# Four graph layers on one core: a 300-wide memset ahead of each gather in five edge passes, 16 TensorE columns in the typed pass, last rows gathered straight into place

## The reference, cut to what matters

```
h = relu(layernorm(x)); x = x + GAT2(GAT1(h))        # attention, 3 heads, then 1
h = relu(layernorm(x)); x = x + log_softmax(RGCN1(RGCN0(h)))   # 8 relation types
h = relu(layernorm(x)); x = x + relu(h + sheaf(h))   # a small MLP per edge
h = relu(layernorm(x)); x = x + typed(h)             # 90 relation types
```

## Time and profile before

| | us |
|---|---|
| Median of 3 runs | 33200.59 |
| Lowest and highest of them | 33169.5, 33225.65 |
| Profiled execution, its time | 33120.21 |
| Its span | 33118.5 |

### The profile page before, as it was taken

The page is one execution under the profiler, slowest core; times in us unless marked ns, Lnnn a source line. Parts: engine busy times, 40 slices in busy tenths (PEclk is TensorE's granted clock), DMA queues, the critical chain, the costliest instruction groups (busy, mean ns, idle before and its releaser), DMA issues. The chain is left out here.

```text
span 33118.5 us, 433539 instructions
## 1 busy us (share of the span) xinstructions
PE 19164.6 (58%) x155012; PEld 15014.2 (45%) x155012; DVE 15783.7 (48%) x40197; ACT 1449.8 (4%) x3069; POOL 20831.6 (63%) x22292
## 2 busy tenths in 40 slices
PE   0565655588884555553777739899898892100000
PEld 0344444244443444443666628888888882000000
DVE  3444444455554444443666636667666663211110
ACT  0000000000000000000000001111111110000000
POOL 2544444566663444444888856888888885577776
PEclk9777777699996777776888869999999995555555
DMA  4111111111111100100111112222222223311111
GB/s 68 43 42 39 41 41 43 25 37 39 37 39 25 22 20 20 22 20 19 28 24 26 24 20 33 38 36 38 38 35 39 38 35 48 77 20 19 19 20 16
DMA packets 1707135, 1084.73 MB, mean 33 GB/s; under 512 B 1291531, under 2 KB 1565931, under 8 KB 1672139
## 3 DMA queue, kind: packets, MB, share of 16 engines
q0 software_dynamic: 934304, 199.11, 9.7%
q1 hardware_dynamic: 661867, 435.33, 5.6%
q10 hardware_dynamic: 110016, 437.07, 3.4%
HBM read 607.13 MB, written 462.62 MB: 32 GB/s over the span
## 5 line engine op out<-in xcount | busy, mean ns | idle before, releaser
L879 PE MATMUL gat_e_found<-gat_e_parts,gat_e_lowhot 128*128 128x266 bf16 (+1 forms) x36456 | 6298.0, 327 | 2542.1 <-issue 2386.8
L692 POOL DMA_INDIRECT rgcn_e_rows<-rel_t,rgcn_e_index x4464 | 4285.4, 960 | 3253.4 <-DMA rgcn_e_rows<-rel_t,rgcn_e_index 2449.1
L2039 POOL DMA_INDIRECT bysrc<-sheaf_e_toadd,sheaf_e_torow x3224 | 5182.0, 1607 | 1356.3 <-issue 862.3
L879 PEld LDWEIGHTS gat_e_found<-gat_e_parts,gat_e_lowhot 128*128 128x128 bf16 x36456 | 3645.3, 101 | 5194.3 <-issue 3397.1
L2278 PE MATMUL sheaf_e_found<-sheaf_e_parts,sheaf_e_lowhot 128*128 128x238 bf16 x46872 | 5310.3, 274 | 1003.3 <-DVE sheaf_e_lowhot L2090 523.7
L961 POOL DMA_INDIRECT gat_e_rows<-att_t,gat_e_index x4712 | 4464.7, 948 | 1999.1 <-issue 1510.8
L2278 PEld LDWEIGHTS sheaf_e_found<-sheaf_e_parts,sheaf_e_lowhot 128*128 128x128 bf16 x46872 | 4699.8, 102 | 1459.8 <-issue 641.5
L1769 PE MATMUL rgcn_e_found<-rgcn_e_parts,rgcn_e_lowhot 128*128 128x224 bf16 x41664 | 4424.5, 271 | 7.1 <-DVE rgcn_e_lowhot L1622 7.1
L1769 PEld LDWEIGHTS rgcn_e_found<-rgcn_e_parts,rgcn_e_lowhot 128*128 128x128 bf16 x41664 | 4163.0, 103 | 548.4 <-issue 398.6
L692 POOL DMA_INDIRECT typed_e_rows<-typed_t,typed_e_index x3224 | 3424.9, 1062 | 1074.1 <-issue 1060.6
L843 DVE TENSOR_TENSOR gat_e_picked<-gat_e_found,gat_e_highhot 128x532 f32<-128x532 f32 (+1 forms) x868 | 763.5, 880 | 4230.8 <-DMA count_rows<-dst_d,count_index 2071.6
(11 more groups left out here) (459 smaller groups left out, 20331.6 us busy)
## 6 DMA issues: line engine op xcount, KB each, us to landing
sheaf_e_allsrc<-src_d ACTq DMA_DIRECT2D x62, 1664.0 KB
sumsatt<-gat_e_sums ACTq DMA_DIRECT2D x62, 1404.0 KB
gat_e_rows<-att_t,gat_e_index POOLq DMA_INDIRECT x4712
typed_t<-typed_p_y SPq DMA_DIRECT2D x98, 765.0 KB
rgcn_e_rows<-rel_t,rgcn_e_index POOLq DMA_INDIRECT x4464
sheaf_e_low<-low_d SPq DMA_DIRECT2D x62, 1152.0 KB
sumsatt<-gat_e_sums ACTq DMA_DIRECT2D x62, 1092.0 KB
rgcn_e_low<-low_d SPq DMA_DIRECT2D x124, 512.0 KB
```

The costliest lines, as they stand in the source:

```text
L692: pool.indirect_dma_start(self.rows[k][:, j, :], None, table, rows(self.index[k][:, j:j + 1]))\
L879: last = pe.matmul(self.found_ps[n % 2][:, c, 0:self.width * NHI], hot[:, k, col * P:(col + 1) * P], self.table.column(part, k), start=par ...
L2039: pool.indirect_dma_start(g.by_src[k][r], rows(to_row[k][:, j:j + 1]), to_add[k][:, j, 0:FD], None, compute_op=ALU.add).then_inc(summed[k] ...
```

## The change

- `Pause.rest` puts a memset of 128x300 on POOL ahead of each gather, with a wait for the memset before it. All five passes use it; the element of gat1, the landing waits of gat2 and rgcn0 and the 400-wide memset of rgcn1 go.
- The typed pass finds 16 of 52 columns on TensorE. A found column gives `h[src]` and the source's part of the weight (17 values); `look` picks the type's 16x16 matrix by a one-hot of the type (3 matmuls of 256 columns per edge column), and `apply` multiplies and reduces on DVE (512 products for two columns). DVE's list for this pass is written anew, in the same form as in gat1.
- `project`: for wide tables ACT copies the first of the three banks. `parts` has two columns, and its store is contiguous (partition-major), with an index `dst_first_p` to fit.
- `gather_to` issues its 98 gathers straight into the result, without DVE; in the sheaf layer they run beside the loads of the eight tables, which DVE adds to each other first.

```diff
+PAUSE = 300
 def gather_to(nc, g, name, table, index, width, into):
-    gather_by_node(nc, g, name, table, index, width, copy, 2)
+            def _(pool):
+                gather_nodes(pool, table, index, width, into, got)
+                pool.wait_ge(got, 16 * NT)
+def gather_nodes(pool, table, index, width, into, got):
+    for t in range(NT):
+        pool.indirect_dma_start(into[:, t, 0:width], None, table, rows(index[:, t:t + 1])).then_inc(got, 16)
...
 # project
-                        for n in range(banks):
+                        for n in range(1 if shares else 0, banks):
...
+                def copy_first(i, k):
+                    act.wait_ge(product[k], i + 2)
+                    act.wait_ge(stored[k], i * 16 + 16)
+                    act.copy(rows_out[k][:, 0, 0:pieces[0][4]], y_ps[k][0][:, 0:pieces[0][4]])\
+                        .then_inc(first_copied[k], 1)
...
-                        sp.dma_start(by_node(node_table), keep[0][:, :, :]).then_inc(by_node_out, 16)
+                    sp.dma_start(node_table.rearrange("(p t) w -> p t w", p=P), keep[0][:, :, :])\
+                        .then_inc(by_node_out, 16)
...
+class Pause:
+    def rest(self, pool, n, first=False):
+        if not first:
+            pool.wait_ge(self.over, n)
+        pool.sem_inc(self.g.gate, 1)
+        pool.memset(self.cells[:, :], 0.0).then_inc(self.over, 1)
...
 # EdgeBuffers.gather_chunk: rgcn0, rgcn1
-            if self.space == "landed" and j > 0 and j % 2 == 0:
-                pool.wait_ge(self.gathered[k], turn * (16 * self.cols) + 16 * j)
-                pool.sem_inc(g.gate, 1)
-            elif self.space == "time":
...
-                pool.memset(self.spacer[:, :], 0.0).then_inc(self.spaced, 1)
+            self.pause.rest(pool, (turn * 2 + k) * self.cols + j, isinstance(turn, int) and turn == 0 and k == 0 and j == 0)
             self.gather_column(pool, table, k, j)
...
 # attention_pass: gat1, gat2
-                        if not kinds:
...
-                            pool.memset(spacer[:, :], 0.0).then_inc(spaced, 1)
-                        elif j % 8 == 0 and j > 0:
-                            pool.wait_ge(gathered[a.k], a.turn * (16 * JG) + 16 * j)
-                            pool.sem_inc(g.gate, 1)
+                        pause.rest(pool, a.c * JG + j, fresh and a.k == 0 and j == 0)
...
 # finish_sheaf
+            def _(pool):
+                gather_nodes(pool, g.sums["sheaf"], g.last_row, FD, agg, got)
...
+                for n in range(1, len(tables)):
+                    dve.wait_ge(in_[n], 16)
+                    o.link(dve.tensor_tensor(total, total, parts[n][:, :, :], ALU.add))
+                dve.wait_ge(got, 16 * NT)
...
+class TypedFinder(Finder):
+    def build_low(self, dve, a, q, fresh=False):
...
+        dve.tensor_scalar(self.type_hot[(a.k * self.groups + q) % 2][:, :],
+                          self.type_rows[a.k][:, q * QC * P:(q + 1) * QC * P], self.g.lane_f[:, :], None, ALU.is_equal)
+        super().build_low(dve, a, q, fresh)
+    def look(self, pe, a, n, first=False):
...
+            for part in range(3):
+                last = pe.matmul(self.kind_ps[n % 2][:, c, :, :].rearrange("p o i -> p (o i)"),
+                                 hot[:, col * P:(col + 1) * P], ...)
+    def apply(self, dve, o, a, n, rows_t, fresh=False):
...
+        o.link(dve.tensor_tensor(self.mapped[:, :, :, :], self.kind_ps[n % 2][:, :, :, :],
+                                 rows_t[a.k][:, j:j + 2, 0:FD].unsqueeze(2).to_broadcast([P, 2, FD, FD]), ALU.mult))
+        dve.tensor_reduce(rows_t[a.k][:, j:j + 2, 0:FD], self.mapped[:, :, :, :], AX.X, ALU.add)\
+            .then_inc(self.applied, 1)
...
 # typed_attention_pass, DVE, in the turn of chunk a (old = a-1)
+                    for n in range(f.halves):
+                            f.fetch(dve, o, a, n, rows_t, first, last)
+                        if fetches and n > 1:
+                            f.apply(dve, o, a, n - 2, rows_t, fresh=first and n == 2)
...
+                        if n == 0: begin(o, old)
+                        elif n == 1: weigh(o, old)
+                        elif n == 2: scale(o, old)      # waits for old's gathers, frees its rows
+                        else: add_up(o, old, n)
```

More of the change, by code:

```diff
@@ L552, in _ @@
                         last.then_inc(turned_sb[k], 1)
+                        if shares and not (first and k == 0):
+                            copy_first(i - 1 + k, 1 - k)
+                turn(0, first=True)
+                with act.Fori(1, turns) as i:
+                    turn(i)
+                if shares:
+                    copy_first(turns - 1, 1)
             @block.sync
@@ L588, in _ @@
                 pool.sem_inc(g.gate, 1)
-                pool.indirect_dma_start(first[:, :], None, node_table, rows(g.dst_first[:, :])).then_inc(got, 16)
+                first_node = g.dst_first_p if put_kept and node_table is not table else g.dst_first
+                pool.indirect_dma_start(first[:, :], None, node_table, rows(first_node[:, :])).then_inc(got, 16)
                 pool.wait_ge(ready, 1)
@@ L1542, in relation_pass @@
     with Stage(nc, name) as s:
-        b = EdgeBuffers(s, g, FD, index_d, extras, FD, JP, "landed" if first else "time")
+        b = EdgeBuffers(s, g, FD, index_d, extras, FD, JP)
         short = SplitTable(s, [h[:, :, :]], FD)
@@ L2611, in _ @@
                 o = Order(dve, dve_o)
+                dve.memset(raw[:, :, :], 0.0).then_inc(cleared, 1)
                 dve.memset(dst_part[1][:, :], 0.0)
[L2613 to L2641 removed]
@@ new lines, in add_up @@
+                def add_up(o, a, step):
+                    k = a.k
+                    if step == 3 and not a.is_first():
+                        dve.wait_ge(stored[k], a.turn * 16)
+                    steps = last_step - 2
+                    for c in range((step - 3) * FD // steps, (step - 2) * FD // steps):
+                        last = scan_sum(dve, sums[k][:, :, c], keep_ps, scaled[:, :, c],
+                                        sums[1 - k][:, J - 1, c:c + 1])
+                    if step == last_step:
+                        o.link(last)
+                        dve.sem_inc(done, 1)
@@ new lines, in _, with turn @@
+                o = Order(dve, dve_o, (NCH // 2 - 2) * per + base)
+                turn(o, At(NCH // 2 - 1, 1), last=True)
+                turn(o, At(NCH // 2, 0), fetches=False)
+            @block.tensor
+            def _(pe):
+                pe.wait_ge(f.table.ready, 1)
+                pe.wait_ge(f.kinds_ready, 1)
+                def turn(a, first=False):
+                    for n in range(f.halves):
+                        f.find(pe, a, n, first)
+                        f.look(pe, a, n, first)
+                turn(At(0, 0), first=True)
+                turn(At(0, 1))
+                with pe.Fori(1, NCH // 2) as i:
+                    for k in range(2):
+                        turn(At(i, k))
```

273 lines of the change are left out of this document (200 added, 73 removed).

## The result

The changed kernel took 29,630.6 us (median of 3, 29,597 to 29,786), the kernel before 33,200.6: ratio 0.893, 95% interval 0.889 to 0.897. The forecast was 28,770. The profiled execution took 29,786, where the sum gave 28,695: 1,091 us are missing, and the traces say where.

A forecast was written before the change was run, and what follows sets the result against it. Gathers on POOL and PE's matmuls, stalled beside rapid gathers, added up in gat1; POOL bound rgcn1. Terms summing to -4425 took the profiled 33,120 to 28,695, hence 28,770 us for the median; range 28,350 to 30,000.

The forecast's parts named there:

- main case: Whole kernel: POOL's pace sets all five passes, 28,770 us, within 28,400 to 29,100; chance 0.68.
- rival B: In gat1 and typed PE is partly held back, losing 12 us a chunk each: 30,260 us; chance 0.10.
- I take full speed: In the five passes PE keeps its full matmul speed at the smallest new gather spacing, 1.475 us.
- Rival A: PE is still held back at 1.475 us spacing in all five passes: 39,600 us, slower than before; chance 0.05.
- The pace: POOL in the passes: 1.519 us a gather, chunk starts included, with a 300-element memset of an estimated 371 ns.
- typed: Typed pass: 58.0 us a chunk at 1.611 us a gather, 3596 us for 4485, a gain of 889.
- lower bound of the pace: Typed pass: 1.519 us a gather instead of 1.611, if the longer gather does not stay; 3390 us.
- Rival C: Typed pass: PE and DVE bound it in turn, 66 us a chunk, 29,270 us in all; chance 0.12.
- Rival D: PE's stalls come from its own two-chunk loop, not from gathers: 32,960 us; chance 0.02.
- Small parts: Outside the passes' main gathers: projection -50, one-word store -50, last rows -66, sheaf -100 us.

The follow-up runs named there:

- first chip: Chip of the main result: kernel before 33,200 us, changed kernel 29,630 us.
- fourth chip: Another chip: kernel before 33,242 us, unchanged changed kernel 29,711 us, ratio 0.893.
- second chip: Another chip: kernel before 33,101 us in its profiled run (elsewhere 33,087), unchanged changed kernel 28,599 us, ratio 0.865.
- third chip: Another chip: kernel before 30,270 us; the changed kernel ran there only with memsets of 400, 350 or 200 elements, or without gathers.
- fifth chip: Another chip: kernel before 30,171 us; one variant of the changed kernel ran there, 28,849 us.
- half: Changed kernel with one-element memsets and gathers of 64 rows instead of 128 in gat1 and gat2 only: 37,248 us.
- p1: Changed kernel with `PAUSE = 1`, the memset before each gather at one element instead of 300: 36,919 us.
- mix: Changed kernel with memsets of 350 elements in gat1, rgcn0, rgcn1 and typed, 300 in gat2: 28,849 us, ratio 0.956 to the kernel before.
- the loop alone: Changed kernel with the five passes' gathers replaced by memsets, the 300-wide memsets kept: 24,857 us.
- 200: Changed kernel with memsets of 200 elements instead of 300: 27,439 us on the third chip, 34,225 us on the fourth chip.
- 350: Changed kernel with memsets of 350 elements instead of 300: 28,947 us on the third chip, 29,108 us on the fourth chip.

## Why the prediction was right, and where not

29,630 us lies in the range of 28,350 to 30,000, the direction was right, and the kernel gained 3,570 us of the 4,430 forecast. The mechanism was right where nothing holds TensorE back: there POOL's pace sets the end of all five passes. But the main case, 28,400 to 29,100 with a chance of 0.68, is not what the first chip did; the range held since it had been drawn over a milder rival B as well, and which chip the kernel met was luck: 28,599 on another, the main case.

Median matmuls a us between neighbouring gathers, by spacing (what a pass takes when nothing holds it: 8.6 to 8.8 in gat1, about 10 in rgcn; "by eights" is with a wait for landing after each eight, and gat2 asks for little more than it gets there):

```
gathers apart   first and fourth chip            second chip         third and fifth chip
1.25 us         0.8 (gat1 before; half: rgcn)    0.8 (p1, all)       not profiled
1.25, by eights 4.8 (gat2 before)                4.8 (gat2 before)   not profiled
1.395-1.399     2.15 (all five passes)           not run             8.6 gat1, 10.0 rgcn
1.478           5.3-5.4 gat1, 5.4 rgcn           8.6 gat1, 6.1 rgcn  4.7 (gat2 of mix)
1.52            8.5 gat1, 7.1-7.2 rgcn           not run             8.5 gat1, 7.9-8.6 rgcn
1.56            8.3 (rgcn1 before)               8.3 (rgcn1 before)  8.3 gat1, 8.3-8.8 rgcn
```

- **The step that failed is "I take full speed"** at 1.475 us, and behind it the thought that a row near to the good one decides. What was lost between 1.25 and 1.56 doesn't come back in proportion: on chips of the first kind the median is 1, 3 and 8 matmuls a gather at 1.25, 1.395 and 1.478 us, and enough only at 1.52. The margin had also to be read against the need: gat2's calm at an average of 1.52 proved little, since it asks for 4.1 matmuls a us and the others for 6.1 to 7.0, and since its landing waits break the run of gathers: without them, at `PAUSE = 1`, it gets 0.8 a us.
- **The price** is the 1,096 us of POOL's waits, 3.6, 4.6, 4.1 and 5.5 us a chunk in gat1, rgcn0, rgcn1 and typed. This is rival B in kind, a partial hold, with other numbers: it had 12 us a chunk in two passes, and it was four passes with a third to a half of that. 30,260 was too long, 28,770 too short.
- **Rival A** did not come true at 1.478 us. Its mechanism, the gathers and then TensorE alone, is there at 1.25 us (`PAUSE = 1`, 36,919 us): 79 to 82 us a chunk and 88 in gat2, where A, with the longer gathers of the pause in it, had 88 to 92 and 102. At 1.395 on the fourth chip the kernel is slower than before, at 71.8 to 75.3 us a chunk.
- **The pace** was right: 1.524 to 1.527 for 1.519, memsets 373 ns for 371.
- **The main case is the second chip's run.** From its own profiled run of the kernel before, 33,101 - 4425 = 28,676; it took 28,591. gat1 -1464 (forecast -1495), rgcn0 -1506 (-1570), rgcn1 -188 (-191), gat2 +14 (-14), typed -1060 (-889).
- **typed**: the longer gather (1.062 us) did not stay: 0.971 at 1.478 us from the same table, 0.972 at 1.395 and 0.947 at 1.25. So it was neither the table nor the pace; in the pass before, with nothing between the gathers, single ones take 0.94 or 1.09, and why is open. The lower bound of the pace was named and not taken, and that cost 187 us. VectorE is busy 2583 us, not 2700; the loop alone takes 43.8 us a chunk, not 48. Rival C is out by that, and by 55.2 us a chunk on the second chip.
- **Rival D** is out: the stalls follow the gathers' spacing in the same loop. The instruction queue in the profile's part 3 moves 680 packets in the changed kernel and 682 in the one with 1.25 us, so it is not more fetching either; whether a fetch takes longer beside the gathers, no run shows. The Trainium skill, Runtime: NRT & Kernel Launch, section Instruction fetch mechanics, says that refills in order are mostly hidden and that branches out of the window stall; the trace agrees as far as the packets go, and the rule has no stall at each gather.
- **Small parts** (second chip): from the last gather of one pass to the first of the next (in sheaf the last scatter), and from typed's last to the end, 2,304 us for 2,622, the stretch ahead of gat1 15 longer: -303, forecast -266. The last rows brought 17, 16 and 29 (22 each), sheaf to typed 152 (200). Missed were 60 and 43 behind gat1 and gat2: before, TensorE still had 60 and 42 us of finds left when POOL had gathered the last chunk (TensorE held back, as in the earlier trace rows). On the first chip these tails came back in rgcn0, rgcn1 and typed (24 to 31 us each), which ate the small parts' gain there.

Two groups of lines on POOL, second chip, between sheaf and typed (count, busy, mean ns, idle before): the last rows' gathers and the wait for the contiguous store:

```profile
L310 POOL DMA_INDIRECT sheafn_agg<-sumssheaf,whole_lastrow x98 | 100.0, 1020 | 32.5 <-issue 29.6 <-PEq L2481 3.0
...
L630 POOL DMA_INDIRECT typed_p_first<-typed_dst,whole_dstfirstp x1 | 1.0, 980 | 8.3 <-DMA typed_dst<-typed_parts 8.3
```

The gathers idle 32.5 us in all where those of the same place idled 51.9 before on this chip, but each takes 1.02 us for 0.946. The store's wait is 8.3 us for 51.2 before on this chip (53.0 on the first): -43, with -50 forecast.

**Open.** What is shared between a gather's start and TensorE's supply of instructions is not known; the runs show only that it does not go by rows or bytes, and that it sets in after some gathers of an unbroken run. Nor is it settled that it is the chip: the second to fifth are four different ones, none met twice, so a condition that lasts as long as a set of runs (rival M) would look the same. Within a set the runs of the kernel before agree within 0.2%. That the third chip's 2,930 us lie in gat1 and rgcn0 is inferred: the kernel before was not profiled there. And which pause is best depends on it: 200 wins by 5% over 350 where nothing is held back (27,439 to 28,947), and loses 18% where it is. 350 is the one tried on both the third and the fourth chip that lets no chunk wait on either; it did not run on the second.

## What to carry to other kernels

When the profile puts an engine's idle time down to `issue` in pieces that repeat with another engine's instruction, count the instructions that it gets in each period, and compare that with what the stage needs: a rate against a need says which stages will suffer, a "good" and a "bad" spacing do not. A pause tuned near such an edge should be tried on several chips, and the margin be priced (here 0.042 us a gather, 1.7% of the time) against what falls off the edge (up to 18%). A duration that differs between two stages (0.97 and 1.06 us) is not yet one of the data; look for its cause, or carry both ends into the sum.

## What the runs showed of the hardware

- Beside an unbroken run of indirect gathers from GpSimd, TensorE gets its instructions late, on some chips: medians of 1, 3 and 8 matmuls a gather at 1.25, 1.399 and 1.478 us (first and fourth chip), and 1 also with 64 rows instead of 128, at 1.21 us (same packets, fewer bytes). The portions come 0.74 us apart at 1.478, half the spacing.
- It takes a few gathers to set in: at 1.25 us the first six of a chunk in gat1 leave 9 to 11 matmuls each, then 0 to 2; with a wait for landing after each eight, gat2 keeps a median of 6.
- The spacing from which it happens differs: 1.478 us is held on the first and the fourth chip and nearly free on the second; 1.395 is free on the third and held on the fourth (1.399). The kernel before took 30,171 to 33,242 us on five chips.
- A gather of 64 rows takes 0.907 us on GpSimd on average (gat1 and gat2 of that run), one of 128 rows 0.950 (the run with 1.25 us): nearly all of its price does not depend on the rows.
